# Attention by batch with transposed scores, and expert tiles started in three phases around the last batch's routing

## The chip, the cores and the metric

The kernel runs on one core of a Trainium2 chip. Its engines are TensorE (PE, with its weight loads listed as PEld), VectorE (DVE), ScalarE (ACT), GpSimd (POOL) and SyncE (SP), and they meet only at semaphores. The metric is the time of one execution on the device in microseconds; the median of three runs is given. All matrices are float32 unless a name ends in _b (bf16).

## The reference

Cross attention over 4 batches of 512 tokens (width 128, 16 heads of 8) with 77 context rows per batch, then a layer of 8 experts with 2 choices per token among 9 (the ninth returns the token itself):

```python
q = (query @ Wq + bq).reshape(b, nq, H, DH).transpose(0, 2, 1, 3)
scores = jnp.einsum('bhqd,bhkd->bhqk', q, k) / np.sqrt(DH)
scores = jnp.where(mask, -jnp.inf, scores)
w = jax.nn.softmax(scores, axis=-1)
attn = jnp.einsum('bhqk,bhkd->bhqd', w, v)
x = x + attn.transpose(0, 2, 1, 3).reshape(b, nq, H * DH) @ Wo + bo   # query = layernorm(x)
logits = xn @ router_w + router_b                                      # xn = layernorm(x)
probs = jax.nn.softmax(logits, axis=-1)
top_v, top_i = jax.lax.top_k(probs, TOP_K)
gates = jnp.sum(jax.nn.one_hot(top_i, E + 1) * top_v[..., None], axis=-2)
h = jax.nn.gelu(jnp.einsum('btd,edf->ebtf', xn, w1), approximate=False)
y = jnp.einsum('ebtf,efd->ebtd', h, w2)
x = x + jnp.einsum('bte,ebtd->btd', gates[..., :E], y) + gates[..., E:] * xn
```

## The kernel before

**Attention** goes by tiles of 128 tokens, 16 of them, four to a batch. For each tile PE writes the scores of 16 heads x 77 keys (1232 columns) into the four banks of ps_s (L774): K is block diagonal (kbd), so that four groups of 32 rows of the array work on four banks. DVE takes the maximum of each head in two halves of 616 columns (mx, L1058) and subtracts it (sc, L1062); ACT takes one exponential of 1232 columns (ex, L665). PE then transposes the 1232 columns in ten pieces (L798), ACT copies them out of PSUM in three parts (exT, L547), and ten products with a block diagonal V that holds a column of ones per head give both the weighted values and the sums (ps_av, L807). DVE multiplies with the reciprocals (L1081, L1082); one more transpose, one copy (L611) and one product with Wo (L786) follow, and DVE adds the residual tile by tile (L1070). The order is written out by hand: at tile i the engines do the scores of i, the transposes and products of i - 1 and the projection of i - 2. The batches in the middle run in a hardware loop.

**Routing** of a batch is spread over the four tiles of the next one: layer norm (ACT L591), transposes (L840), logits (L849), DVE's choice of two experts (choose, L1092 to L1107), ranks by triangular bf16 products (L861 to L867), slots (place, L1116 to L1128). POOL sends each tile's 128 rows twice, once per chosen expert, with an indirect DMA into the table slots in DRAM (send, L480), eight to a batch. The last batch is routed in two parts after its attention, with no other work beside it.

**Expert stage.** DVE works out a table of 40 tiles of 128 rows (L1190 to L1204: which expert, which row of slots). SP writes four pads of zero rows into slots and ACT four more (write_pad, L317 and L318), one per expert, at the end of its rows. SP then waits for the pads and for all sends, and loads tile after tile (xg, L364), eight buffers deep. For each tile PE transposes the rows (L917), multiplies with w1 (four products, each of two instructions, L926), ACT takes the gelu (L701), PE multiplies with w2 (L935), DVE scales by the gate (yg, L1222) and POOL scatters the result to pairs (L523). DVE also copies the expert's w1 to a fixed place (L1215) and the transposed rows out of PSUM (L1208). PE's order at step j is gather_t(j), up(j - 1), down(j - 2). At the end SP reads pairs back, DVE adds the two halves and the residual (L1246, L1247), and SP stores the result.

## Time and profile before

| what | value |
|---|---|
| median of 3 runs | 248.63 us (248.18 to 250.15) |
| profiled execution, span from first to last instruction | 257.3 us |
| busy: PE, DVE, POOL, ACT | 191.6, 156.0, 102.4, 102.0 us |
| start, to the first reduction of scores | 25.0 us |
| attention with routing of batches 0 to 2 | 25 to 135 us |
| routing of the last batch, table, pads, first load | 135 to 160.4 us |
| expert tiles | 160.4 to 242 us |
| last scatter, pairs, sum, store | 242 to 257.3 us |

The span of the one profiled execution is 8.7 us above the median of the runs without a profile; of the profiled execution only its span is recorded, with no time of its own around it. Busy shares are means over stages with different limits, so each stage is to be read by itself.

### The profile page before, as it was taken

Reading aid. Unit: us, or ns where it says so; the run is one execution under the profiler, and the core shown is the slowest. Engines: PE = TensorE matmul, PEld = TensorE weight load, DVE = VectorE, ACT = ScalarE, POOL = GpSimd, SP = SyncE. Lnnn points to the kernel's source line nnn. Section 1 sums busy time; section 2 is a strip of 40 time slices with the busy share of each in tenths; the row PEclk is TensorE's granted clock in tenths of the full one; section 3 lists DMA queues with packets and bytes.
Section 4 is the critical chain, followed back from the end, with each engine's and each line's share of the span. In section 5 each row is a group of like instructions: output and inputs, shape, how many; then the busy total and the mean of one; then the engine's idle time right before and its main releaser. Section 6 shows DMA issues by size and latency. Waiting matters only on the chain.

```text
span 257.3 us, 5658 instructions
## 1 busy us (share of the span) xinstructions
PE 191.6 (74%) x1467; PEld 169.9 (66%) x1468; DVE 156.0 (61%) x498; ACT 102.0 (40%) x210; POOL 102.4 (40%) x148
## 2 busy tenths in 40 slices
PE   1747899999986599849783200999999999999500
PEld 0516488778765587739782100899999999999500
DVE  2799968788883678938853650254554554554226
ACT  2411565678654476436653310122322322323100
POOL 8293001002047520782057479044554554554600
PEclk9999999999999589997978555599999999999955
DMA  3535892000001000110001031212222222210069
GB/s 98 159 122 215 263 309 83 4 0 0 4 20 44 9 0 0 37 36 0 0 28 50 21 103 50 61 47 74 59 68 64 71 62 68 62 52 11 3 218 271
DMA packets 20303, 18.30 MB, mean 71 GB/s; under 512 B 3255, under 2 KB 16752, under 8 KB 20287
## 3 DMA queue, kind: packets, MB, share of 16 engines
q1 hardware_dynamic: 16831, 13.98, 18.5%
q0 software_dynamic: 2304, 3.75, 4.7%
q10 hardware_dynamic: 1152, 0.37, 0.6%
q8 instruction: 8, 0.13, 0.2%
q14 instruction: 8, 0.07, 0.1%
HBM read 10.60 MB, written 8.50 MB: 74 GB/s over the span
## 4 chain that ended last, share of the span: by engine, by line
PE 48%; DVE 23%; issue 9%; DMA 6%; ACT 4%; another core or an unknown queue 4%; SPq 3%; POOL 1%; DVEq 0%; POOLq 0%; ACTq 0%
PE ps_s L926 14%; PE ps_av L807 8%; PE ps_av L935 7%; PE ps_o L935 6%; PE ps_t L798 5%; DVE mx L1058 4%; DVE sc L1062 3%; DMA pair_sb<-pairs 2%; PE ps_t L917 2%; DMA ctx_sb<-in_ctx 2%; DVE v_sb L1030 1%; PE ps_s L774 1%; DVE v_sb L1032 1%; SPq L317 1%
## 5 line engine op out<-in xcount | busy, mean ns | idle before, releaser
L523 POOL DMA_INDIRECT pairs<-yg,xg x40 | 39.1, 976 | 44.1 <-issue 22.7
L701 ACT ACTIVATE hT<-ps_s 128x512 f32<-128x512 f32 x40 | 23.9, 597 | 61.5 <-PE ps_s L926 61.5
L480 POOL DMA_INDIRECT slots<-rows,slot x32 | 31.7, 990 | 39.1 <-issue 18.3
L926 PE MATMUL ps_s<-xgT,w_now 128*128 128x128 f32 x320 | 44.4, 283 | 0.0
L807 PEld LDWEIGHTS ps_av<-vbd,exT 128*128 128x128 f32 x320 | 40.9, 205 | 2.4 <-issue 2.4
L807 PE MATMUL ps_av<-vbd,exT 128*128 128x99 f32 (+1 forms) x320 | 41.8, 286 | 0.8 <-issue 0.8
L926 PEld LDWEIGHTS ps_s<-xgT,w_now 128*128 128x128 f32 x320 | 40.5, 199 | 0.1
L1215 DVE COPY w_now<-w_sb 128x512 f32 x40 | 17.2, 429 | 21.5 <-issue 16.9
L798 PE MATMUL ps_t<-ident,ex 128*128 128x128 f32 x160 | 28.1, 314 | 0.1
L547 ACT COPY exT<-ps_t 128x384 f32<-128x384 f32 (+1 forms) x48 | 24.1, 514 | 7.5 <-PE ps_t L798 4.2
L1058 DVE TENSOR_REDUCE mx<-ps_s 128x8 f32<-128x616 f32 x32 | 25.4, 793 | 2.5 <-PE ps_s L774 1.9
L1062 DVE TENSOR_TENSOR sc<-ps_s,mx 128x616 f32<-128x616 f32 x32 | 25.6, 799 | 1.3
L665 ACT ACTIVATE ex<-sc 128x1232 f32<-128x1232 f32 x16 | 19.7, 1230 | 10.2 <-DVE sc L1062 10.1
L436 POOL TENSOR_TENSOR kbd<-kT,hm 128x308 f32<-128x308 f32 x4 | 2.8, 704 | 51.9 <-PE ps_s L774 46.8
L798 PEld LDWEIGHTS ps_t<-ident,ex 128*128 128x128 f32 x160 | 20.9, 160 | 2.6 <-ACT ex L665 0.8
L917 PE MATMUL ps_t<-ident,xg 128*128 128x128 f32 x40 | 11.5, 287 | 14.6 <-DMA xg<-slots 14.5
L935 PE MATMUL ps_av<-w_sb,hT 128*128 x160 | 22.2, 283 | 0.0
L935 PE MATMUL ps_o<-w_sb,hT 128*128 x160 | 21.5, 277 | 0.2 <-issue 0.2
L935 PEld LDWEIGHTS ps_av<-w_sb,hT 128*128 128x128 f32 x160 | 20.2, 198 | 0.2
L935 PEld LDWEIGHTS ps_o<-w_sb,hT 128*128 128x128 f32 x160 | 19.5, 192 | 0.4 <-issue 0.4
L774 PE MATMUL ps_s<-kbd,qT 32*128 32x308 f32 x128 | 16.7, 510 | 2.9 <-DVE sc L1062 1.6
L1208 DVE COPY xgT<-ps_t 128x128 f32<-128x128 f32 x40 | 11.4, 284 | 8.3 <-PE ps_t L917 8.3
(157 smaller groups left out, 239.9 us busy)
## 6 DMA issues: line engine op xcount, KB each, us to landing
xg<-slots SPq DMA_DIRECT2D x40, 65.0 KB
pairs<-zeros SPq DMA_DIRECT2D x4, 512.0 KB, 4.0
w_sb<-in_L_ffn_w SPq DMA_DIRECT2D x1, 2048.0 KB, 9.7
pair_sb<-pairs SPq DMA_DIRECT2D x3, 512.0 KB, 4.7
x_sb<-in_x SPq DMA_DIRECT2D x4, 256.0 KB, 6.7
out<-out_sb SPq DMA_DIRECT2D x3, 256.0 KB, 2.9
pairs<-yg,xg POOLq DMA_INDIRECT x40
slots<-rows,slot POOLq DMA_INDIRECT x32
```

What stands on the lines that cost most here:

```text
L480: pool.indirect_dma_start(slots, bass.IndirectOffsetOnAxis(ap=slot[k][:, t, c:c + 1], axis=0), rows[:, t, :], None, bounds_check=ROWS - 1, ...
L523: pool.indirect_dma_start(pairs, bass.IndirectOffsetOnAxis(ap=xg[:, u, D + 1:D + 2].bitcast(U32), axis=0), yg[:, u % 4, :], None, bounds_c ...
L547: act.copy(dst, src).then_inc(t_used, 1)
L665: act.activation(ex[:, t % 2, 0:HK], sc[:, t % 2, :], ACT.Exp).then_inc(ex_ready, 1)
L701: act.activation(hT[:, u % 2, :], ps_h[u % 2], ACT.Gelu).then_inc(h_used, 1)
L774: m = pe.matmul(ps_s[:, g, 0:GK], qT[r, P * t:P * (t + 1)], kbd[r, :, :].rearrange("p h k -> p (h k)"), start=True, stop=True)
L798: m = pe.transpose(ps_t[bank][:, P * (c - a):P * (c - a + 1)], ex[:, par, P * c:P * (c + 1)], ident[:, :])
L807: m = pe.matmul(ps_av[:, (DH + 1) * head0[c]:(DH + 1) * head0[c] + VC], exT[:, par, P * c:P * (c + 1)], v, start=c == 0, stop=c == NCH - 1 ...
L926: m = pe.matmul(ps_h[par][:, P * c:P * (c + 1)], w1_now[:, par, P * c:P * (c + 1)], xgT[:, par, :], start=True, stop=True)
L935: m = pe.matmul(ps_y[par], hT[:, par, P * c:P * (c + 1)], w2_sb[:, bass.ds(e + P * c, D)], start=c == 0, stop=c == FC - 1)
L1058: link(dve.tensor_reduce(m, s, AX.X, ALU.max))
L1062: dve.tensor_tensor(o.rearrange("p (g h k) -> p g h k", g=2, k=NK), s, m.rearrange("p (g h) -> p g h", g=2).unsqueeze(3) .to_broadcast([P, ...
```

## The change

The kernel is rewritten in most of its functions; the expert tile itself (gather_t, up, gelu, down, take_result, send_back) keeps its instructions.

- **Scores twice.** For each batch the scores are still computed with tokens on the partitions, but only to take their maxima (max_scores on PE into one pair of banks ps_m, top_scores on DVE). The maxima of a batch are split into three bf16 parts (split), transposed (max_out) and copied out (mT_out). Then score_t writes the scores of the whole batch transposed, keys on the partitions and 512 tokens in the free dimension, in three rounds of up to 103 rows of the 308 (4 heads x 77 keys) per group: first a bf16 product that puts minus the maximum into PSUM, then kbd times q on top. ACT's exponential writes exT straight from PSUM. The transposes of ex, their copies, and DVE's subtraction are gone.
- **Products by column groups.** attend multiplies exT (512 columns) with 32 columns of V for each of four groups, each to its own 32 partitions of one bank, and the same again with ones (den). inverse (ACT: Ln, Exp) and combine (DVE, one Newton step) give the transposed attention output; project and residual go by batch.
- **The start.** Context and weights come packed and transposed from the host side, constants come by DMA instead of from POOL; the batch's maxima of batch 0 are taken ahead of the loop.
- **Three phases.** The table is made in parts: tiles 0 to 7 after the routing of batches 0 and 1, tiles 8 to 15 after batch 2 (full tiles only), tiles 16 to 38 after batch 3 and the pads, which SP now writes alone (eight). NJ goes from 40 to 39. PE starts expert tiles right behind the attention of the last batch, whose remaining steps (combine, project, residual, norm, logits, choose, ranks, place, table, send) stand between expert tiles 1 to 8. xg has 16 buffers, yg has 8. All loops are unrolled.

The diff, cut to its core (a gap is marked by a line of three dots):

```diff
+NJ = NTOK * TOPK // P + E - 1
...
+NR = 3
+CUT = [0, 103, 206, 308]
...
+PHASES = [(0, 8), (8, 16), (16, NJ)]
+XR = 16
+YR = 8
...
-
-            sp.wait_ge(tab_ready, 1)
-            for e in range(E // 2):
-                write_pad(sp, e)
-            sp.wait_ge(tab_ready, 2)
-
...
+            for q, (a, z) in enumerate(PHASES):
+                for b in range(q + 2 if q < 2 else B):
+                    sp.wait_ge(sent[b], 16 * 2 * TT)
+                if q == 2:
+                    sp.wait_ge(pad_ready, 1)
+                    for e in range(E):
+                        row = sp.value_load(tab_pad[0:1, e:e + 1], min_val=0, max_val=DEAD - P)
+                        sp.dma_start(slots[bass.ds(row, P), :], padrows[:, :]).then_inc(pads_done, 16)
+                    sp.wait_ge(pads_done, 16 * E)
+                sp.wait_ge(tab_ready, q + 1)
+                for i in range(a, z):
+                    load(i)
...
+            for i in range(NJ):
+                send_back(i)
+                if i == 1:
+                    b = B - 1
+                    pool.wait_ge(stats2_ready, B)
+                    pool.wait_ge(rstd2_ready, 1)
+                    pool.tensor_tensor(rstd2[:, b * TT:NT], veps2[:, b * TT:NT], seed2[:, b * TT:NT],
+                                       ALU.pow).then_inc(rstd2_ready, 1)
+                if i == 2:
+                    prepare(B - 1)
+                if i == 3:
+                    pool.wait_ge(lgx_ready, B)
+                    pool.tensor_tensor(lex[:, :, :], r0[:, 0:TT * (E1 + 2)].rearrange("p (t e) -> p t e", t=TT),
+                                       lgx[:, :, :], ALU.pow).then_inc(lex_ready, 1)
+                if i == 5:
+                    send(B - 1)
+                if i == 24:
+                    identity(2)
+                if i == 30:
+                    identity(3)
...
+                for h in range(2):
+                    act.wait_ge(s_full, 2 * n + h + 1)
+                    act.activation(exT[0:w, n % ES, 2 * h:2 * h + 2, :], ps_s[0:w, 2 * h:2 * h + 2, :],
+                                   ACT.Exp).then_inc(s_free, 1)
...
+            for i in range(NJ):
+                gelu(i)
+                if i == 2:
+                    norm2(B - 1)
+                if i == 3:
+                    x2nT_out(B - 1)
+                if i == 4:
+                    logits_out(B - 1)
+                if i == 6:
+                    ranks_out(B - 1)
...
+            def max_scores(b, t):
+                for h in range(2):
+                    begin_m(f"d {b} {t} {h}")
+                    scores(b, t, h, ps_m).then_inc(m_full, 1)
...
+            def score_t(b, r):
+                n = NR * b + r
+                w = CW[r]
+                if r == 0:
+                    pe.wait_ge(mT_ready, b + 1)
+                if n:
+                    pe.wait_ge(s_free, 2 * n)
+                for g in range(G):
+                    pe.matmul(ps_s[0:w, g, :], ind_b[32 * g:32 * g + 12, CUT[r]:CUT[r + 1]],
+                              mT[32 * g:32 * g + 12, b % 2, :], start=True, stop=False)
+                for g in range(G):
+                    flat = kbd[32 * g:32 * g + 32, b, :, :].rearrange("p h k -> p (h k)")
+                    m = pe.matmul(ps_s[0:w, g, :], flat[:, CUT[r]:CUT[r + 1]], qT[32 * g:32 * g + 32, b % 3, :],
+                                  start=False, stop=True)
+                    if g % 2:
+                        m.then_inc(s_full, 1)
...
+            def attend(b, r):
+                n = NR * b + r
+                w = CW[r]
+                if r == 0:
+                    av, den = begin_v(f"av {b}"), begin_v(f"den {b}")
+                av, den = ps_v[v_use(f"av {b}")[0]], ps_v[v_use(f"den {b}")[0]]
+                pe.wait_ge(s_free, 2 * n + 2)
+                for g in range(G):
+                    i = pe.matmul(av[32 * g:32 * g + 32, :], vbd[0:w, r, b, g, :], exT[0:w, n % ES, g, :],
+                                  start=r == 0, stop=r == NR - 1)
+                if r == NR - 1:
+                    v_filled(i, f"av {b}")
+                for g in range(G):
+                    i = pe.matmul(den[32 * g:32 * g + 32, :], dbd[0:w, r, b, :], exT[0:w, n % ES, g, :],
+                                  start=r == 0, stop=r == NR - 1)
+                if r == NR - 1:
+                    v_filled(i, f"den {b}")
+                else:
+                    i.then_inc(av_rounds, 1)
+
...
+                score_t(b, 0)
+                if b == 0:
+                    fill_xn(1)
+                    fill_v(1)
+                    fill_q(1)
+                    fill_v(2)
+                    pe.wait_ge(bv4_ready, 1)
+                    v_filled(pe.matmul(begin_v("bo")[:, 0:D], bv4[:, :], wo_sb, start=True, stop=True), "bo")
+                    pe.wait_ge(kbd_ready, B)
+                    bank, k = v_use("q 1")
+                    pe.wait_ge(v_free[bank], k + 1)
+                if b >= 1:
+                    attend(b - 1, 1)
+                    attend(b - 1, 2)
                 for t in range(TT):
+                    if b + 1 < B:
+                        max_scores(b + 1, t)
+                    if t == 0:
+                        score_t(b, 1)
+                    if t == 1 and b >= 1:
+                        project(b - 1)
+                    if t == 1 and b + 2 < B:
+                        fill_xn(b + 2)
+                    if t == 2:
+                        score_t(b, 2)
+                    if t == 2 and b + 2 < B:
+                        fill_q(b + 2)
+                if b >= 1:
+                    fill_x2n(b - 1)
+                    logits(b - 1)
+                if b == 0:
+                    pe.wait_ge(dbd_ready, 1)
+                    pe.wait_ge(vbd_ready, NR)
+                attend(b, 0)
+                if b + 1 < B:
+                    max_out(b + 1)
+                if b >= 1:
+                    ranks(b - 1)
+                if b + 2 < B:
+                    bank, k = v_use(f"q {b + 2}")
+                    pe.wait_ge(v_free[bank], k + 1)
+            attend(B - 1, 1)
+            attend(B - 1, 2)
...
-                def transposes(p):
-                    number, bank = fill(kind, n, FILLS[f"T{t}"] + p)
-                    begin_fill(number)
-                    a, z = PIECES[p]
-                    for c in range(a, z):
-                        m = pe.transpose(ps_t[bank][:, P * (c - a):P * (c - a + 1)], ex[:, par, P * c:P * (c + 1)],
-                                         ident[:, :])
-                    m.then_inc(t_full, 1)
-
-                def products(p):
-                    number, _ = fill(kind, n, FILLS[f"T{t}"] + p)
-                    pe.wait_ge(t_used, number + 1)
-                    for c in range(*PIECES[p]):
-                        v = vflat[:, bass.ds((b * NCH + c) * VC, VC)]
-                        m = pe.matmul(ps_av[:, (DH + 1) * head0[c]:(DH + 1) * head0[c] + VC],
-                                      exT[:, par, P * c:P * (c + 1)], v, start=c == 0, stop=c == NCH - 1,
-                                      skip_group_check=True)
-                    return m
-
-                pe.wait_ge(ex_ready, i + 1)
-                transposes(0)
-                transposes(1)
-                if project_before:
-                    project(i - 1, (par + 1) % 2)
-                transposes(2)
-                if isinstance(i, int) and i == 0:
-                    pe.wait_ge(vbd_ready, 3)
-                else:
-                    pe.wait_ge(av_ready, i)
-                products(0)
-                if last_tile and kind != "last":
-                    number, bank = fill(kind, n, FILLS["q"])
-                    fill_q(number, bank, fill(kind, n, FILLS["xn"])[0])
-                products(1)
-                if last_tile and kind == "mid":
-                    ranks(n - 1)
-                products(2).then_inc(av_full, 1)
...
+            for i in range(NJ + 2):
+                if i < NJ:
+                    gather_t(i)
+                if 1 <= i < NJ + 1:
+                    up(i - 1)
+                if i == 2:
+                    project(B - 1)
+                if i == 5:
+                    fill_x2n(B - 1)
+                if i == 6:
+                    logits(B - 1)
+                if i == 8:
+                    ranks(B - 1)
+                if i >= 2:
+                    down(i - 2)
...
+            def split(b):
+                parts = [mpad[:, :, i, :] for i in range(3)]
+                m = mx[:, :].rearrange("p (a j) -> p a j", j=HG)
+                rest = [mrest[:, i, :].rearrange("p (a j) -> p a j", j=HG) for i in range(2)]
+                link(dve.tensor_copy(parts[0], m))
+                link(dve.tensor_tensor(rest[0], m, parts[0], ALU.subtract))
+                link(dve.tensor_copy(parts[1], rest[0]))
+                dve.tensor_tensor(parts[2], rest[0], parts[1], ALU.subtract).then_inc(split_ready, 1)
...
+            def combine(b):
+                av, den = ps_v[v_use(f"av {b}")[0]], ps_v[v_use(f"den {b}")[0]]
+                dve.wait_ge(r0_ready, b + 1)
+                wait_v_full(dve, f"den {b}")
...
-            def less_max(kind, n, t):
-
-                i = n * TT + t
-                par = t % 2
-                for half in range(2):
-                    dve.wait_ge(s_full, i * 2 + half + 1)
-                    s = ps_s[:, 2 * half:2 * half + 2, 0:GK].rearrange("p g (h k) -> p g h k", k=NK)
-                    m = mx[:, par, 8 * half:8 * half + 8]
-                    link(dve.tensor_reduce(m, s, AX.X, ALU.max))
-                    if half == 0 and (kind != "first" or t >= 2):
-                        dve.wait_ge(ex_ready, i - 1)
-                    o = sc[:, par, 2 * GK * half:2 * GK * (half + 1)]
-                    dve.tensor_tensor(o.rearrange("p (g h k) -> p g h k", g=2, k=NK), s,
-                                      m.rearrange("p (g h) -> p g h", g=2).unsqueeze(3)
-                                      .to_broadcast([P, 2, HG, NK]), ALU.subtract).then_inc(s_used, 1)
...
+                    if b + 1 < B:
+                        top_scores(b + 1, t)
+                    if t == 0 and b >= 1:
+                        combine(b - 1)
+                    if t == 1 and b >= 1:
+                        residual(b - 1)
+                    if t == 2 and b >= 1:
+                        refine2(b - 1)
+                if b + 1 < B:
+                    split(b + 1)
+                    mT_out(b + 1)
+                if b >= 1:
+                    choose(b - 1)
+                    place(b - 1)
+                if b == 2:
+                    table(0)
+                if b == 3:
+                    table(1)
...
+            for i in range(NJ + 2):
+                if i < NJ:
+                    if i == PHASES[phase_of(i)][0]:
+                        dve.wait_ge(tab_ready, phase_of(i) + 1)
+                    take_w1(i)
+                    take_rows(i)
+                if i >= 2:
+                    take_result(i - 2)
+                if i == 1:
+                    combine(last)
+                if i == 2:
+                    residual(last)
+                    ts = slice(last * TT, NT)
+                    dve.memset(seed2[:, ts], -0.5)
+                    link(dve.memset(r0[:, 0:TT * (E1 + 2)], float(np.e)))
+                    dve.tensor_scalar(veps2[:, ts], mv2[:, ts, 1], EPS, None, ALU.add).then_inc(rstd2_ready, 1)
+                if i == 3:
+                    refine2(last)
+                if i == 6:
+                    choose(last)
+                if i == 8:
+                    place(last)
+                    table(2)
```

## Rows read from the trace of the kernel before

**Rows 1.** Stretches of the span (busy us per engine, granted clock, DMA share, GB/s)
```profile
77.00:106.00 29.00, 23.74 (x180) 20.29 (x180) 19.88 (x63) 15.65 (x34) 12.35 (x18) 0.88 0.05 17
135.00:160.40 25.40, 3.62 (x22) 2.51 (x22) 9.99 (x61) 5.80 (x18) 17.72 (x23) 0.59 0.19 57
160.40:242.00 81.60, 80.49 (x680) 79.33 (x680) 38.62 (x119) 23.90 (x40) 37.92 (x40) 0.96 0.21 55
242.00:257.30 15.30, 0.00 (x0) 0.00 (x0) 5.93 (x11) 0.00 (x0) 1.68 (x2) 0.60 0.67 206
```

**Rows 2.** Chain that ended last: two pauses that no recorded instruction releases
```profile
80.26 5.39 another core or an unknown queue
...
110.65 4.01 another core or an unknown queue
```

**Rows 3.** Timeline of the start
```profile
15.67 1.41 PE L774 MATMUL ps_s<-kbd,qT 32*128 32x308 f32 x8 [1.04 <-ACT qT L552]
...
21.52 0.84 DVE L970 BATCH_NORM_STATS2 st<-x_sb 128x6 f32<-128x128 f32 x4
```

**Rows 4.** Groups by line and shape (busy us, mean ns of one, idle before)
```profile
L1058 DVE TENSOR_REDUCE mx<-ps_s 128x8 f32<-128x616 f32 x32 | 25.4, 793 | 2.5 <-PE ps_s L774 1.9 <-issue 0.3
...
L665 ACT ACTIVATE ex<-sc 128x1232 f32<-128x1232 f32 x16 | 19.7, 1230 | 10.2 <-DVE sc L1062 10.1
...
L1246 DVE TENSOR_TENSOR out_sb<-pair_sb 128x512 f32<-128x512 f32 x3 | 2.1, 691 | 6.9 <-DMA pair_sb<-pairs 6.9
```

**Rows 5.** Timeline of PE within a batch
```profile
43.27 1.05 PE L742 MATMUL ps_t<-xnT,wq_sb 128*128 128x512 f32 x2
...
45.79 0.80 PE L774 MATMUL ps_s<-kbd,qT 32*128 32x308 f32 x8
```

**Rows 6.** Timeline of DVE: routing of one batch, table of 40 tiles
```profile
96.92 0.19 DVE L1092 TENSOR_TENSOR lgx<-lg_sb,rb_sb 128x36 f32<-128x36 f32 x1
...
98.75 0.20 DVE L1106 TENSOR_TENSOR chosen<-oh 128x36 bf16<-128x36 f32 x1
...
147.67 0.16 DVE L1189 CAST tab_pad<-nextrow 128x8 int32<-128x8 f32 x1
...
151.18 0.18 DVE L1204 TENSOR_SCALAR tab_row<-jrow 128x40 int32<-128x40 f32 x1
```

**Rows 7.** Timeline of the expert stage: two neighbouring tiles on PE, one on DVE
```profile
200.02 0.27 PE L917 MATMUL ps_t<-ident,xg 128*128 128x128 f32 x1
...
201.06 0.43 DVE L1215 COPY w_now<-w_sb 128x512 f32 x1 [0.48 <-issue]
...
201.40 0.29 DVE L1208 COPY xgT<-ps_t 128x128 f32<-128x128 f32 x1
...
201.92 0.27 PE L917 MATMUL ps_t<-ident,xg 128*128 128x128 f32 x1
...
202.12 0.35 DVE L1222 TENSOR_SCALAR yg<-ps_av,xg 128x128 f32<-128x128 f32 x1 [0.43 <-PE ps_av L935]
```

**Rows 8.** Timeline of POOL: rows sent to the slots, the last tile sent back
```profile
76.72 0.97 POOL L480 DMA_INDIRECT slots<-rows,slot  x1 [0.30 <-issue]
78.00 0.98 POOL L480 DMA_INDIRECT slots<-rows,slot  x1 [0.30 <-issue]
...
243.12 0.97 POOL L523 DMA_INDIRECT pairs<-yg,xg  x1 [0.41 <-issue]
245.35 2.55 SPq L376 DMA_DIRECT2D pair_sb<-pairs  x5
```

**Rows 9.** Timeline of SP and ACT queues: pads, then the first seven loads
```profile
148.85 7.66 SPq L318 DMA_DIRECT2D slots<-padrows  x4
149.09 2.64 ACTq L318 DMA_DIRECT2D slots<-padrows  x3
...
158.54 7.47 SPq L364 DMA_DIRECT2D xg<-slots  x7
```

**Rows 10.** Chain that ended last: a load from its issue to its landing
```profile
159.68 1.74 DMA xg<-slots
```

1572 lines of the change are left out of this document (713 added, 859 removed).

## The prediction

> **What bounds the kernel now.** I read the stretches first [rows 1]. In a batch of attention (77 to 106 us) PE is busy 23.7 of 29.0 us and DVE 19.9: neither is full, so the chain between them sets the time. From 135 to 160.4 us PE works 3.6 us: the last batch is routed with nothing beside it, and this is the hole that the change aims at. From 160.4 to 242 us PE is full, a tile every 1.90 us [rows 7], and DVE needs 0.48 + 0.43 + 0.28 + 0.35 = 1.5 us of each 1.9 (the wait for the register before w_now, and the three instructions). Then the chain of what ended last: it holds two pauses of 5.4 and 4.0 us in which no recorded instruction releases anybody [rows 2]. They sum to 9.4, and the profiled span is 8.7 above the median of the timed runs. I therefore take the pauses for the profile's own: 257.3 - 9.4 = 247.9 stands for 248.6, and my sum, which has no such pauses, is compared with 247.9, with 0.7 added at the end.
>
> **The start.** Before, the first scores begin at 15.7 [rows 3]. The context transposes and the V product ahead of it go, and DVE writes the normalised rows: I put the first scores at 12.9. The first reduction starts at 14.1; eight of 0.79 [rows 4] and three groups of statistics (0.84 for four tiles [rows 3], with the aggregation 1.25) give 24.2; the second refinement, split, the transposes and the copy of the maxima some 3.3: batch 0's maxima are there at **27.5**.
>
> **Prices on PE.** A 512-column pass takes (1.05 - 0.19) / 2 = 0.43, where 0.19 is the time from a matmul's last column to its end; eight passes of 308 columns in four row groups take 0.80 - 0.19 = 0.61 [rows 5], where one after another they would take 8 x 0.26 = 2.1. So score_t costs 1.0 for kbd times q (0.61 x 512 / 308) and 0.25 for the bf16 part: 1.25. A half of max_scores has two groups: 0.75 until DVE sees it. attend uses column groups, which no row of this trace shows. Its bounds: as good as row groups, 2 x 1.0 = 2.0; one after another, 16 x 0.43 = 6.9. I take 2.0, as the row groups show the array's other direction at work, and keep 6.9 as a rival. The Trainium skill (TensorE: Matmul & The Clock Gate, part 3) has three column groups of 512 columns at 2.38 times one; by that attend would be some 2.9, and 12 of them 11 us more in all; no row here shows it.
>
> **A batch of attention after the change** (b = 2), from the copied maxima on. PE waits for choose of batch 0 (96.92 to 98.95, 2.0 [rows 6]) and does its ranks: 2.4. score_t 3.65, attend twice 7.65. Then the first two halves: ps_m is one pair of banks, so PE's fill of 0.75 and DVE's 0.79 take turns: 10.8. combine, three steps of 0.69 [rows 4]: 12.9. Two reductions with a fill between them: 15.3; residual with statistics 2.2: 17.5; two reductions 19.9; refine2 20.9; two reductions 23.3, split 24.2. Beside it the third score_t ends at 20.3, ACT's exponentials take 2 x 1.02 (1.23 x 1024 / 1232 [rows 4]), the norm 1.95, the transposes, their copy, the logits 2.3: 26.6. attend 2.0 and the maxima's transposes and copy 1.05: **29.6**. Batch 1 has no ranks to wait for but a q copy: 27.9. Batch 0, with V, q and xn of batch 1 ahead of the first exponential: 21.2. Batch 3 has no maxima: 2.4 + 1.25 + 4.0, inverse, exponentials, combine and project to 12.1, score_t and residual to 14.3, third exponential 17.0, norm and logits 21.6, choose 23.7, ranks and two attends **28.0**. So the expert tiles begin at 27.5 + 21.2 + 27.9 + 29.6 + 28.0 = **134.2**, where they began at 160.4 (151.0 without the pauses). What goes per tile (ten transposes, the copies, 1.6 us of subtraction) was real work, but the new chain has the maxima's turns in its place: the attention with its last routing gains 17 us, no more.
>
> **The expert stage.** PE's own work is 39 x 1.90. But DVE, in order, carries the last batch between tiles. DVE is in table(1) until 1.9 after PE's first tile. Nine tile steps at 1.2 are 10.8, seven results 2.5, combine 2.1, residual 2.8, choose 2.3, place 1.6, and some 5.8 of waits: POOL's power behind two scatters (1.6), gelu and down behind the norm (1.4), down behind project, logits and ranks (2.8). The slots are there at 1.9 + 22.1 + 5.8 = 29.8. Behind place stands table(2) (3.7 for 40 tiles [rows 6]), during which PE idles. POOL then sends eight times, one each 1.28, the last landing 2.2 after its start [rows 8]: 41.1. Only then does SP write pads, eight on one queue. Price of one: 1.07 as a load (7.47 / 7 [rows 9]), or 2.1 as the pads of before (7.66 for four starts and the ACT queue at the same time); I take 1.2, since the slow ones coincide with ACT's pads, which are gone: 50.7. Landing 1.7, then a load of 0.6 + 1.74 [rows 10]: tile 16 is there at 54.7. PE could have taken it at 46: it **stands still for 8 to 9 us**. From there 23 x 1.90 + 2.8 = 46.5, and one tile's time (1.9) for a clock that has fallen in the pause, as it has to 0.59 from 135 to 160.4 [rows 1]: 103.1, against 81.6 now. Everything that hides sends and pads of the last batch is 15 tiles of 1.9; the waits above have used it up before they start.
>
> The Trainium skill (DMA: Bandwidth & Descriptors, on issuing engines) says that DMAs from several engines share the same 16 DMA engines, so that a second issuer saves only issue time; by that, moving four pads from ACT to SP costs just four issues, 4.8 of my 9.6. The rows speak rather for two issuers being slower each (2.1 against 1.07 [rows 9]), and the sum would be the same.
>
> **The end** is unchanged, 15.3 [rows 1]. identity of batches 2 and 3 lies between scatters in POOL's slack (1.28 of 1.90).
>
> **The sum.** 134.2 + 103.1 + 15.3 = 252.6, and 0.7: **253.3**, 1.9% slower. Under 1% a measurement here hardly tells from no change.
>
> **Rivals.**
> 1. *The chain loosens* (27%). Before, a batch takes (29.0 - 5.4) / 19.9 = 1.2 times its busiest engine. After, DVE has 17.2 us of work in a batch and PE some 18 to 19. With 1.2 times 18.5, batches 1 to 3 would take 22.2 and not 28.5 on average: 19 us less, and a start that is 3 us shorter: **231**. It needs PE to fill ps_m while DVE is still busy elsewhere. Against it: the two halves of one tile can't overlap, and attends, score_t and norm stand in line.
> 2. *Pads stay slow* (17%), slower than before: eight at 2.1 and not 1.2 move tile 16 by 7 us: **260**. It decides from 1.2 us a pad up. For it: the rows of before. Against: two issuers then, one now.
> 3. *Column groups do not overlap* (7%): 4.9 more for each of 12 attends, little of it hidden since three of them stand in the chain of every batch: about **305**.
> 4. *The phases don't start early* (7%): if sends or table of batches 1 and 2 are late, PE waits at tile 0 or 8. Sends of batch 1 end some 17 us into the last batch, well ahead of its 28; I add 3 to 5 us: **257**.
>
> **How the numbers follow.** The forecast has 42%; around it I allow 246 to 260 (start and batches 1.5 us each, pads from 1.07), of which 6% are faster by over 1%, 12% within it, 24% slower. With the rivals: faster 6 + 25, within 1% 12 + 2, slower 24 + 17 + 7 + 7, rounded to 0.31, 0.14, 0.55. The range 231 to 264 leaves out rival 3 and the far half of rival 1.
>
> **What the new profile would show.** The first expert transpose near 134 (rival 1: under 120). A gap on PE before the 17th tile, with SP's pads in it and a load as what ends it: 8 us, or 15 under rival 2. A smaller gap near tile 9 while DVE makes the table. attend's 16 passes within 2 us, or 7. DVE waiting for PE and PE for DVE in turns at each pair of maxima, and DVE busy well under 20 us a batch. If PE has no gap of over 3 us ahead of tile 16, the step of the pads is wrong; if a batch takes under 25 us, that of the turns is; if pauses like those two are in no run without a profile, my basis holds.

## The result, and the profile after

| | before | after |
|---|---|---|
| median | 249.39 us (4 runs, 248.18 to 254.4) | 289.26 us (4 runs, 287.85 to 290.3) |
| ratio | 1 | 1.158 (1.149 to 1.168) |
| span of the profiled execution | 257.3 us | 286.4 us (288.45 in all) |

The change makes the kernel 16% slower. I had forecast 253.3 us, with a range from 231 to 264. Medians and ranges here hold every execution; the ratios leave out those that took over 1.5% longer than the quickest of the same kernel.

The page of after: span, busy shares, and the clock in 40 slices of 7.2 us.

```profile
span 286.4 us, 4468 instructions
PE 201.5 (70%) x1299; PEld 133.9 (47%) x1299; DVE 131.8 (46%) x463; ACT 76.7 (27%) x135; POOL 108.8 (38%) x133
...
PEclk9995585559795796555955977996697799999955
```

The stretches of after, beside [rows 1]: busy us by engine, granted clock, DMA share, GB/s. The cuts lie at the ends of the four copies of maxima (mT), the first expert transpose, the transpose of tile 16 and the end of PE's work (rounded; the table of the miss has them exactly).

```profile
0.00:28.10 28.10, 12.85 (x52) 6.29 (x52) 18.57 (x70) 5.31 (x12) 9.15 (x24) 0.87 0.68 225
28.10:61.50 33.40, 27.65 (x118) 12.07 (x118) 10.68 (x21) 11.41 (x18) 4.93 (x4) 0.60 0.22 62
61.50:93.70 32.20, 25.56 (x146) 11.31 (x146) 12.33 (x31) 11.00 (x18) 0.86 (x3) 0.78 0.00 1
93.70:129.00 35.30, 26.14 (x146) 11.72 (x146) 15.43 (x55) 10.39 (x18) 12.23 (x16) 0.68 0.04 14
129.00:161.10 32.10, 22.82 (x149) 8.33 (x149) 17.61 (x97) 10.59 (x20) 12.87 (x18) 0.66 0.12 32
161.10:221.00 59.90, 37.31 (x280) 35.76 (x277) 27.27 (x112) 13.68 (x25) 38.39 (x34) 0.84 0.17 52
221.00:270.00 49.00, 48.83 (x414) 48.30 (x414) 23.91 (x69) 14.33 (x24) 28.40 (x33) 0.95 0.19 51
270.00:286.40 16.40, 0.36 (x4) 0.17 (x2) 6.03 (x11) 0.00 (x0) 1.94 (x2) 0.61 0.64 192
```

Read the clock column first. From 28 to 161 us it is 0.60 to 0.78, where before had 0.88 in a batch with one of its two pauses [rows 1] and the full clock in the 29 us of attention ahead of them:

```profile
43.00:72.00 29.00, 28.17 (x238) 23.30 (x237) 23.89 (x75) 21.20 (x44) 1.52 (x4) 1.00 0.01 2
```

The clock has two levels, 1.2 and 2.4 GHz, so 0.60 means that it stood at the lower one for four fifths of batch 0. The miss, term by term:

| term | forecast | measured | miss |
|---|---|---|---|
| batch 0's maxima there | 27.5 | 28.1 | +0.6 |
| batch 0 | 21.2 | 33.4 | +12.2 |
| batch 1 | 27.9 | 32.2 | +4.3 |
| batch 2 | 29.6 | 35.4 | +5.8 |
| batch 3, to the first expert transpose | 28.0 | 32.0 | +4.0 |
| tile 16 after the start of the tiles | 54.7 | 59.5 | +4.8 |
| from there to PE's end | 48.4 | 49.8 | +1.4 |
| the end | 15.3 | 16.0 | +0.7 |
| sum | 252.6 | 286.4 | +33.8 |

27 of 34 us lie in the attention. What the level does to one operation is seen where it changes within a batch. Timeline of PE in after: start, duration, then the name; each row is eight passes in four column groups.

```profile
89.44 1.94 PE L671 MATMUL ps_v<-exT,vbd 103*32 103x512 f32 x8
91.15 1.74 PE L676 MATMUL ps_v<-exT,dbd 103*32 103x512 f32 x8
...
98.31 1.58 PE L671 MATMUL ps_v<-exT,vbd 103*32 103x512 f32 x8
99.72 1.03 PE L676 MATMUL ps_v<-exT,dbd 103*32 103x512 f32 x8
100.58 1.04 PE L671 MATMUL ps_v<-exT,vbd 102*32 102x512 f32 x8
101.44 1.03 PE L676 MATMUL ps_v<-exT,dbd 102*32 102x512 f32 x8
```

An attend is two such rows: 100.58 to the start of the next work at 102.40 is 1.8 us, 89.44 to 92.83 is 3.4 us. The work is the same. The clock fell between 85 and 86 us, behind waits of PE for the last maxima (0.90 us) and the normed rows (0.25); after the wait for the chosen experts (2.55 us, to 95.8) the work was at the low level again, and the high one came back between 99 and 100 us, in the middle of score_t and the attends, which follow each other without a gap from 96.0 on. So the question for the experiments: is the attention long because PE's waits take its clock away, or are the waits themselves the length and the clock only their shadow?

In the expert stage, the timeline of POOL, where the last batch's exponentials are made with a power:

```profile
186.09 7.43 POOL L434 TENSOR_TENSOR lex<-r,lgx 128x44 f32<-128x44 f32 x1 [2.93 <-DVE lgx L971]
193.72 1.04 POOL L417 DMA_INDIRECT pairs<-yg,xg  x1 [0.20 <-issue]
195.06 0.98 POOL L417 DMA_INDIRECT pairs<-yg,xg  x1 [0.31 <-issue]
196.35 0.98 POOL L388 DMA_INDIRECT slots<-rows,slot  x1 [0.30 <-issue]
```

and what PE waited for at two places there (in brackets the idle time and its releaser), then the chain into tile 16:

```profile
200.15 2.08 PE L813 MATMUL ps_s<-xgT,w_now 128*128 128x128 f32 x8 [8.75 <-DVE xgT L1103]
220.63 0.48 PE L805 MATMUL ps_m<-cf,xg 128*128 128x128 f32 x1 [6.54 <-DMA xg<-slots]
```

```profile
216.38 1.69 DMA slots<-padrows
218.09 0.28 SPq L306
218.41 0.15 SPq L306
218.56 0.05 issue
218.81 1.77 DMA xg<-slots
```

DVE stands in place until the power is done, makes table(2) behind it, and PE stands behind DVE for 8.75 us, more than at tile 16; I had forecast a gap there that is smaller than that at tile 16. Then the forecast's gap: eight sends to 205.4, landed at 207.7, eight pads of 1.08 each to 216.4, landing 1.69, load 1.77, and PE idle for 6.54 us ahead of tile 16.

### The profile page after: what moved, and what is told of

The parts are those of the page before. It is cut to its first block, busy times and chain, and to the rows that moved or that the text cites. A ratio compares the mean times of both kernels' runs of the same rounds, so it can differ in the third digit from the quotient of the medians.

```text
span 286.4 us, 4468 instructions
## 1 busy us (share of the span) xinstructions
PE 201.5 (70%) x1299; PEld 133.9 (47%) x1299; DVE 131.8 (46%) x463; ACT 76.7 (27%) x135; POOL 108.8 (38%) x133
## 4 chain that ended last, share of the span: by engine, by line
PE 50%; DVE 18%; issue 12%; DMA 6%; ACT 5%; POOL 4%; SPq 3%; DVEq 1%; POOLq 0%; ACTq 0%
PE ps_s L813 9%; PE ps_s L823 7%; PE ps_m L627 6%; PE ps_v L671 5%; PE ps_s L658 5%; PE ps_v L676 4%; DVE mx L868 4%; DMA exT<-pairs 2%; PE ps_m L714 2%; PE ps_v L687 2%; PE ps_v L614 2%; ACT rows L509 2%; PE ps_v L620 2%; POOL pairs L417 2%; PE ps_v L607 1%
## 5 line engine op out<-in xcount | busy, mean ns | idle before, releaser
L417 POOL DMA_INDIRECT pairs<-yg,xg x39 | 38.5, 987 | 35.2 <-DVE yg L1115 29.1
L823 PE MATMUL ps_s<-w_sb,hT 128*128 x312 | 43.9, 287 | 0.0
L823 PEld LDWEIGHTS ps_s<-w_sb,hT 128*128 128x128 f32 x312 | 40.5, 203 | 0.1
L627 PE MATMUL ps_m<-kbd,qT 32*128 32x308 f32 x108 | 28.4, 612 | 16.6 <-DVE mx L868 15.8
L868 DVE TENSOR_REDUCE mx<-ps_m 128x8 f32<-128x616 f32 x27 | 21.6, 799 | 39.7 <-PE ps_m L627 36.2
L486 ACT ACTIVATE exT<-ps_s 103x1024 f32<-103x1024 f32 (+1 forms) x24 | 23.4, 1020 | 26.9 <-PE ps_s L658 26.7
L1115 DVE TENSOR_SCALAR yg<-ps_s,xg 128x128 f32<-128x128 f32 x39 | 13.6, 349 | 28.3 <-PE ps_s L823 28.3
L377 POOL COPY rows<-rows 128x512 f32<-128x512 f32 x4 | 2.5, 616 | 54.7 <-ACT rows L509 54.7
L658 PE MATMUL ps_s<-qT,kbd 32*103 32x512 f32 (+1 forms) x96 | 23.1, 861 | 0.0
L671 PE MATMUL ps_v<-exT,vbd 103*32 103x512 f32 (+1 forms) x96 | 18.2, 842 | 0.0
L676 PE MATMUL ps_v<-exT,dbd 103*32 103x512 f32 (+1 forms) x96 | 16.6, 774 | 0.0
L805 PE MATMUL ps_m<-cf,xg 128*128 128x128 f32 x39 | 11.3, 295 | 6.5 <-DMA xg<-slots 6.5
```

Of the source, the lines that this page charges most:

```text
L417: pool.indirect_dma_start(pairs, bass.IndirectOffsetOnAxis(ap=xg[:, i % XR, D + 1:D + 2].bitcast(U32), axis=0), yg[:, i % YR, :], None, bo ...
L486: act.activation(exT[0:w, n % ES, 2 * h:2 * h + 2, :], ps_s[0:w, 2 * h:2 * h + 2, :], ACT.Exp).then_inc(s_free, 1)
L627: m = pe.matmul(o[:, g, 0:GK], qT[rows, b % 3, P * t:P * (t + 1)], kbd[rows, b, :, :].rearrange("p h k -> p (h k)"), start=True, stop=True)
L658: m = pe.matmul(ps_s[0:w, g, :], flat[:, CUT[r]:CUT[r + 1]], qT[32 * g:32 * g + 32, b % 3, :], start=False, stop=True)
L671: i = pe.matmul(av[32 * g:32 * g + 32, :], vbd[0:w, r, b, g, :], exT[0:w, n % ES, g, :], start=r == 0, stop=r == NR - 1)
L676: i = pe.matmul(den[32 * g:32 * g + 32, :], dbd[0:w, r, b, :], exT[0:w, n % ES, g, :], start=r == 0, stop=r == NR - 1)
```

## The experiments

Ratios are to the kernel before, run on the same chip in the same group; before took 258.6, 252.4, 259.4 and 253.0 us in the four groups. A batch runs from one copy of the maxima to the next, times and clock from the profile.

**1 and 2. Filler at TensorE's waits** (the second with twice the products at each). The kernel uses all of PSUM, so the products go to places that are rewritten before they are read: a bank of ps_s whose scores are consumed, the next destination, the second bank of ps_m between two uses.

```
+            def warm(o, n):
+                for _ in range(n):
+                    pe.matmul(o[:, 0:256], ones_b[:, :], ind_b[:, 0:256], start=True, stop=True)
...
+                    if h:
+                        pe.wait_ge(s_free, 2 * (NR * (b - 1) + (0, 1, 1, 2)[t]) + 1)
+                        warm(ps_s[:, 0, :], 4)
                     begin_m(f"d {b} {t} {h}")
...
+                warm(o, 4 if b < B - 1 else 0)
                 pe.wait_ge(row_ready, b + 1)
```

> Filler bf16 products of 256 columns (four each, eight before the ranks) stand ahead of TensorE's waits in the attention: the second half of each pair of maxima, the transposed maxima, the normed rows, the transposed rows, the chosen experts. They write PSUM that is overwritten before it is read. Theory A (the attention of after is long because TensorE is at its half clock for most of it: granted 0.66 to 0.74 between 28 and 162 us, and the same 16 passes of attend take 3.4 us there against 1.72 us where it is full): the clock of that stretch rises above 0.8 and the kernel loses 8 to 20 us. Theory B (the turns between TensorE and VectorE alone set the length, the low clock is only their shadow): a filler adds work to a chain that waits, so the time stays within 2 us or grows by up to 4 us, whatever the clock does.

> The same with twice the filler (eight products, sixteen before the ranks), some 0.9 us of it at the full clock and 1.7 us at the half one at each wait. Theory A: the clock of 28 to 162 us above 0.9; 15 to 25 us off the kernel if the fillers don't overhang the waits; where they do (0.9 us of filler in a gap of 0.9 us) they give a few us of it back. Theory B: slower than the light filler, 0 to 8 us over the kernel after.

Measured: 284.07 us, ratio 1.102 (1.092 to 1.111), and 287.04 us, 1.105 (1.095 to 1.115). The four batches of the light one:

```profile
28.50:57.30 28.80, 26.22 (x138) 12.86 (x138) 10.64 (x20) 11.32 (x18) 4.92 (x4) 0.82 0.24 65
57.30:84.10 26.80, 22.55 (x170) 10.39 (x170) 12.32 (x30) 11.00 (x18) 0.87 (x3) 1.00 0.00 1
84.10:115.20 31.10, 26.60 (x182) 13.03 (x182) 15.82 (x56) 10.50 (x18) 12.27 (x16) 0.84 0.05 16
115.20:147.70 32.50, 24.69 (x176) 11.32 (x176) 17.28 (x96) 10.60 (x20) 13.12 (x18) 0.79 0.12 31
```

In batch 1 PE has 24 products more than in after (170 against 146) and is busy 22.6 us instead of 25.6, in a batch that takes 26.8 instead of 32.2. In the two profiles the attention is 14 us shorter (119.2 against 133.0), and theory B, by which added work shortens nothing, is out. The kernel gains less than its attention: 4 to 5% by the ratios of the two runs of after (1.158 and 1.145), but only 2% by the times themselves, 284.07 against 289.26, which are from different chips. Its expert stage is 7 us longer than in after (132.0 against 125.3), and PE stands still for 3.9 of them in one of the pauses of the last section. The full dose reaches no more than the light one, below theory A's 15 to 25 us: its batches 2 and 3 took 35 us each at 0.85 and 0.81, each with a pause of 2.8 or 2.7 us that no recorded instruction ends (last section).

**3 and 4. The two stalls of the expert stage, one at a time.** The pads ahead of the wait for the sends:

```
-                for b in range(q + 2 if q < 2 else B):
-                    sp.wait_ge(sent[b], 16 * 2 * TT)
                 if q == 2:
                     sp.wait_ge(pad_ready, 1)
                     for e in range(E):
...
+                for b in range(q + 2 if q < 2 else B):
+                    sp.wait_ge(sent[b], 16 * 2 * TT)
+                if q == 2:
                     sp.wait_ge(pads_done, 16 * E)
```

> The eight pad writes of the last phase are issued before SyncE waits for the sends of the last batch, not behind them. Both theories: the stall of 6.5 us ahead of tile 16 shrinks. The pads took 8.7 us of issues behind the sends plus 1.7 us of landing; without them the loads start about 10 us earlier than in after, which is more than the stall, so 6 to 7 us come off if what follows is set by TensorE, less if the result transfers of GpSimd are next in line (then 2 to 4 us).

and the exponentials on ScalarE, behind ranks_out(B - 1), with the power on GpSimd taken out:

```
                 if i == 6:
                     ranks_out(B - 1)
+                    router_exp(B - 1)
```

> The last batch's exponentials (128x44) go back to ScalarE's Exp, between two gelus; GpSimd's power of 7.43 us goes. Theory A and B alike: the slots are ready 5 to 7 us earlier, VectorE's wait in place (8.75 us of TensorE idle behind it) falls to 2 to 4 us, two table loads of some 1.3 us each come on ScalarE between the gelus: 3 to 6 us faster. If the stall only moves to tile 16, whose rows wait for the sends, most of it still comes off, since the sends start earlier by the same amount.

Measured: 296.71 us, ratio 1.138 (1.130 to 1.147), and 294.24 us, 1.139 (1.132 to 1.146); some 5 us each against after's 1.158. Against the 1.145 of the second run of after (experiment 5) neither gain is clear of the noise. In the first, PE had no gap at tile 16. But another stood before it, and no recorded instruction ends it; the chain of waits and PE's row:

```profile
211.08 8.01 another core or an unknown queue
```

```profile
220.88 2.08 PE L814 MATMUL ps_s<-xgT,w_now 128*128 128x128 f32 x8 [4.93 <-DVE xgT L1104]
```

Such pauses, like those of [rows 2], are in both kernels and not in after; I come back to them in the last section. This one takes back in full what the pads gave, and they make the two single gains less sure still. In the second, ScalarE needed 1.28 + 0.24 + 1.28 us for table, exponentials and table back, instead of 7.43, and PE's wait fell from 8.75 to 3.57 us, as expected; tile 16 did not come earlier (61.5 us after the first tile, 59.5 in after), with a wait of PE for such a pause, 3.9 us, and one behind the table loads, 1.8 us, on the way. The gain of both together is seen in experiment 8, which has no pause.

**5. After once more,** to have it beside the next three.

> The kernel after, unchanged, beside the kernels of this group, since the kernel before took 258.6 us beside the first four against 249.4 beside after: a ratio of 1.15 to 1.17 again by every theory, and batches of 32 to 36 us at a granted clock of 0.6 to 0.8.

289.22 us, ratio 1.145 (1.139 to 1.150); batches of 32.7, 36.3, 34.6 and 34.2 us at 0.60, 0.65, 0.70 and 0.70.

**6. Maxima bank by bank.**

```
+                both = name[0] == "d" and M_USES[n - 1][0] == "d"
                 if n:
-                    pe.wait_ge(m_free, n)
+                    pe.wait_ge(m_free, n - 1 if both else n)
...
-                    begin_m(f"d {b} {t} {h}")
-                    scores(b, t, h, ps_m).then_inc(m_full, 1)
+                    for g in range(2):
+                        begin_m(f"d {b} {t} {h} {g}")
+                        rows = slice(32 * (2 * h + g), 32 * (2 * h + g) + 32)
+                        pe.matmul(ps_m[:, g, 0:GK], qT[rows, b % 3, P * t:P * (t + 1)],
+                                  kbd[rows, b, :, :].rearrange("p h k -> p (h k)"), start=True,
+                                  stop=True).then_inc(m_full, 1)
```

> The maxima by single PSUM banks: TensorE fills bank 1 while VectorE reduces bank 0 (one matmul and one reduce of 308 columns each), instead of both filling and reducing a pair of banks in turn. No filler. Theory A (the low clock costs most): the waits of 0.9 to 2.2 us behind each pair go, the clock of 28 to 129 us rises, and both together give 8 to 16 us. Theory B (only the turns cost): some 0.7 us less for each of 24 halves that stand in the chain, but VectorE pays about 0.1 us more for each half: 5 to 12 us, and the clock has no say; the passes of attend stay at 3.4 us. Theory C (what stands in line besides the maxima sets the batch: score_t, attends, combine, norm, logits, choose): under 4 us.

289.31 us (285.3 to 290.8) against 289.22 (287.9 to 292.6): no clear gain. In a pair, the two products stand in different rows of the array and run at once: the four passes of a half took 0.79 us. Released one by one they took 1.17 at the full clock (71.8 us). VectorE's halves then followed each other every 1.36 us instead of 1.69 (at 67 and at 69 us of the two traces), and the kernel shows nothing of it. Batch 1 took 32.8 us at 0.75, among the others, so by the time alone this is theory C's "under 4". It doesn't say that the maxima are cheap, as the next run shows.

**7. No maxima after batch 0.** max_scores and top_scores are left out for batches 1 to 3.

> It leaves out part of the computation: the maxima of batches 1 to 3 (24 halves of scores on TensorE and their reductions on VectorE); batch 0's maxima are subtracted in every batch. It prices the maxima with their turns. By the forecast's own batches (each half 1.6 us of turns, partly beside other work) 24 halves come to at most 38 us, of which some 20 to 25 come off. Theory A: TensorE then has even less to do between its waits, so the clock stays at 0.6 to 0.75 and batches 0 to 2 end at 22 to 26 us each, 20 to 28 us off the kernel. Theory B: 30 us or more come off. Theory C: under 12 us.

259.98 us, ratio 1.031 (1.027 to 1.036): 29 us less than after in the same group, more than theory A allowed and just under B's 30.

```profile
28.40:46.90 18.50, 13.37 (x86) 6.53 (x86) 7.22 (x12) 11.01 (x18) 4.93 (x4) 0.89 0.35 98
46.90:72.60 25.70, 18.68 (x114) 7.89 (x114) 5.98 (x22) 10.99 (x18) 0.87 (x3) 0.75 0.00 1
72.60:101.60 29.00, 19.34 (x114) 7.41 (x114) 9.87 (x48) 10.15 (x18) 11.77 (x16) 0.63 0.05 16
101.60:135.90 34.30, 24.83 (x148) 8.88 (x148) 19.19 (x104) 10.71 (x20) 15.01 (x20) 0.70 0.12 34
```

The 24 halves cost 14, 11 and 6 us in the three batches. Theory A had the clock at 0.6 to 0.75 and the batches at 22 to 26 us: batch 0 came to 18.5 us at 0.89, so less work between the waits did not lower the clock there, and batch 2 still took 29.0 at 0.63. So the maxima's turns are not the only waits that go with the low clock. A kernel without them still doesn't beat before.

**8 and 9. Everything together.**

> Bank by bank, the light filler at the waits for the transposed maxima, normed rows, transposed rows and chosen experts (none at the maxima), the pads ahead of the sends, the exponentials on ScalarE, twelve result buffers instead of eight, and GpSimd's sends of the last batch one result later. Theory A: the clock of the attention above 0.85, the expert tiles begin near 140, the stalls before tiles 10 to 16 fall from 15 to about 6 us: 25 to 32 us less than after, a ratio of 1.02 to 1.06 to the kernel before. Theory B: 12 to 18 us less. Theory C: 8 to 14 us, all of it in the expert stage.

> The light filler of the first experiment (four products at the second half of each pair of maxima too) on the kernel with pads ahead of the sends, exponentials on ScalarE, twelve result buffers and the later send. The last combination without a filler at the maxima (and by single banks) had a ratio of 1.07 to the kernel before: attention until 155.6, and 112.4 us from the first expert tile to the end. Theory A (the clock): the attention ends near 148 as with the light filler alone, the clock there is 0.8 to 0.9, the expert stage is the same 112 to 114: 7 to 9 us less, a ratio of 1.03 to 1.05. If the gains of filler and order are the same slack counted twice, it stays at 1.06 to 1.08.

The first: 269.8 us, ratio 1.070 (1.064 to 1.075), 19 us less than after, between the theories: A wanted 25 to 32 us and a clock above 0.85, and the four batches had 0.67, 0.83, 0.75 and 0.83; B allowed 12 to 18. The tiles began at 155.6, where A had 140, and took 112.4 us to the end, against 124.4 in after of the same group: 12 us from pads, exponentials, buffers and the later send, 9.4 of them up to tile 16, which came 49.2 us after the first tile and not 58.5, without a wait. The second: 278.35 us, ratio 1.070 (1.062 to 1.078), where I expected 1.03 to 1.05. Its first two batches were quick, 25.7 us at 0.86 and 27.6 at 0.94; the last two were not, 35.0 at 0.80, with a pause of 3.4 us in it, and 35.2 at 0.71; and its expert stage took 124 us with a pause of 6.5 us in it. The first version had none, so the two are not cleanly comparable.

**10 and 11. The last batch routed ahead of the tiles,** the other half of the change undone (the calls for batch B - 1 moved in front of the loops over tiles on all engines).

> The other half of the change undone: the last batch is combined, routed and sent in one piece ahead of the expert tiles, as in the kernel before (its exponentials on ScalarE, as there); tiles 0 to 15 then run while it is sent and padded. From the end of the last attends some 16 to 18 us pass until place is done, with TensorE nearly idle; then 16 tiles of 1.9 and the table of 3.6. Sends, pads and the load take 10.3 + 2.3 + 8.7 + 1.7 + 2.3 = 25 us beside them, so tile 16 doesn't wait: it comes 50 to 53 us after the end of the attends, where it came 59.8 after it in after. Routing between the tiles is then worth less than nothing: 7 to 10 us faster than after, ratio 1.11 to 1.13. If the waits between tiles were cheap and only power and pads cost, this is slower than after or within 2 us of it.

> Routing first with the light filler in the attention, the pads ahead of the sends and twelve result buffers. The parts should add: 13 us from the filler, 7 to 10 from the order, nothing from the pads, which are hidden already: 20 to 23 us less than after, ratio 1.06 to 1.08. Against the kernel with filler and routing between tiles it tells which order is better once both have no pad stall: by the sums 3 to 5 us in favour of routing between the tiles.

293.9 us, ratio 1.134 (1.127 to 1.141), where I expected 1.11 to 1.13; and 280.42 us, with executions from 275.8 to 286.7 beside 259.4 of before, too far apart for a ratio (1.06 to 1.11). In the first, 52.6 us pass from the last copy of maxima to the first tile, and 105.9 from there to the end: 158.5, against 157.4 in after, but with a pause of 4.2 us in it. Tile 16 has no gap and comes 57.2 us after the end of the attends (166.5), against 59.5 in after; I had written 50 to 53. The waits of PE that remain are those of the routing in one piece, and table(2):

```profile
170.58 2.04 PE L677 MATMUL ps_v<-w_sb,avT 128*128 128x128 f32 x8 [4.13 <-DVEq L908]
178.15 1.08 PE L684 MATMUL ps_v<-cf,rows 128*128 128x128 f32 x4 [5.53 <-ACT rows L502]
...
199.30 1.64 PE L807 MATMUL ps_s<-xgT,w_now 128*128 128x128 f32 x8 [4.13 <-issue]
```

With the filler the two orders have spans of 276.1 and 276.4 us, with pauses in both. So these runs show no gain of the routing between the tiles over the routing in one piece, and none the other way that is clear of the pauses. The three phases let tiles start before the last batch's rows are in place, and either order lets 16 tiles cover its sends.

**12. V later in batch 0.** fill_v(1), fill_v(2) and the product for bo behind the first and second pair of maxima, on PE and DVE alike.

> Only batch 0 is changed: the V products for the second and third range of keys and the product for bo are issued behind the first and second pair of batch 1's maxima instead of ahead of them. In after they stand in the chain with 1.7 + 0.9 us on TensorE and 2 us on VectorE ahead of the first reduction. If the 33 us of batch 0 (21.2 forecast) are a chain of fixed work ahead of the first maxima, 3 to 5 us go from batch 0 and from the kernel. If they are the low clock (0.60 there), the work is only moved and under 2 us go.

305.98 us, ratio 1.169 (1.156 to 1.182), against 1.158 and 1.145 of after: at least it got no faster, and both expectations are missed. Batch 0 shows more:

```profile
28.40:66.60 38.20, 32.03 (x118) 13.79 (x118) 9.53 (x21) 11.51 (x18) 4.93 (x4) 0.51 0.18 50
```

The same instructions, 4.8 us more than in after and 5.8 more than in experiment 10, whose batch 0 is that of after and ran in the same group (32.4 at 0.62); PE is at its lower level throughout. A chain of fixed work would have become shorter. That the solid work between the waits had kept up what clock there was is my reading; no second run tests it.

**13 and 14. Filler in one batch, and more of it at the long waits.**

> The light filler in one batch alone, the one between the second and the third copy of maxima (61 to 94 us in after): four products at the second half of each of its pairs, at the transposed maxima, the normed rows and the transposed rows. Theory A (the clock): this batch alone rises from a granted clock of 0.65 to 0.78 to 0.95 or more and falls from 32 to 36 us to 27 or 28; the batches ahead of it and behind it stay at 32 to 37 us and 0.60 to 0.70. In the sum 5 to 8 us off the kernel. If something else in the filler kernels made them faster (another order at the waits for freed scores, a faster chip), the gain isn't bound to this batch.

> The version with filler and order, with ten products instead of four at the long waits (transposed maxima, normed rows, transposed rows; twenty before the ranks), since its last two batches were still at 0.80 and 0.71 of the full clock and took 35 us each. Over the batches measured so far a batch's time falls by some 3 us for each 0.1 of clock. If the clock of these two rises to 0.9, 3 to 5 us each come off, less about 1 us for filler that overhangs: ratio 1.04 to 1.06 to the kernel before. If the filler overhangs as in the full dose, it stays at 1.07 or gets worse.

The executions of these two spread too far for a ratio: 282.0 to 290.7 us and 264.1 to 276.5, beside 253.0 of before. The batches of the first:

```profile
28.50:60.10 31.60, 26.05 (x122) 11.54 (x122) 10.62 (x20) 11.41 (x18) 4.93 (x4) 0.68 0.22 61
60.10:88.90 28.80, 25.72 (x171) 12.06 (x170) 12.34 (x31) 11.01 (x18) 0.87 (x3) 0.88 0.00 1
88.90:122.60 33.70, 24.44 (x146) 11.34 (x146) 15.50 (x55) 10.39 (x18) 11.93 (x16) 0.71 0.05 15
122.60:154.70 32.10, 22.84 (x148) 8.28 (x148) 17.59 (x96) 10.59 (x20) 12.96 (x18) 0.66 0.12 32
```

Only the batch with filler is at 0.88 and under 29 us, short of the 0.95 and the 27 to 28 us that I expected; its neighbours are at 0.68 and 0.71, as in kernels without filler. That is within one execution, so the chip doesn't explain it. The added wait for freed scores stands in the same batch as the filler; it can only hold PE back, but a kernel with that wait and without the products was not run. In the second kernel the last two batches came to 31.2 and 31.9 us at 0.89, 3 to 4 us less each, as theory A says, while batch 1, with 42 products more than in after, fell to 0.72 and took 36.0: the filler makes the high level likelier, not certain. Its execution of 264.1 us (1.04 times before, the only one in the range that I expected) had a mean clock of 0.894, that of 276.5 us (1.09) 0.837. No version beats before.

The batches of all profiles, each as time at granted clock (without those of experiment 7, and batch 3 without 10 and 11, which route it otherwise):

| batch | in order of clock |
|---|---|
| 0 | 38.2 at 0.51; 33.4 and 32.7 at 0.60; 32.4 at 0.62; 31.2 at 0.67; 31.6 at 0.68; 33.1, 32.7 and 32.8 at 0.69; 28.8 at 0.82; 25.9 at 0.85; 26.1 and 25.7 at 0.86; 25.7 at 0.87 |
| 1 | 36.3 at 0.65; 34.0 (three) and 33.9 at 0.70; 36.0 at 0.72; 32.8 at 0.75; 32.2 at 0.78; 30.8 at 0.83; 28.7 and 28.8 at 0.88; 28.7 and 27.6 at 0.94; 26.8 at 1.00 |
| 2 | 35.4 at 0.68; 34.6 and 35.0 at 0.70; 33.7 at 0.71; 34.3 and 34.0 at 0.75; 31.1 at 0.84; 31.2 at 0.89; with a pause in it: 36.8 (two) at 0.67; 37.9 at 0.68; 34.9 at 0.76; 35.0 at 0.80; 34.9 at 0.85 |
| 3 | 32.0, 32.1 and 34.8 at 0.66; 34.2 at 0.70; 30.9 at 0.83; 31.9 at 0.89; with a pause in it: 34.8 at 0.66; 37.5 at 0.68; 34.2 at 0.70; 35.2 at 0.71; 32.5 at 0.79; 35.2 at 0.81 |

## Why the prediction was wrong

**The step that failed is "Prices on PE".** Each price there is read from rows at the full clock, and the batches add them up as if the chain they form would run at it. I used the clock at one place only, one tile's time after the stall. I named turn-taking between PE and DVE as what sets a batch, and did not ask what turn-taking does to PE's clock, though [rows 1] show it fall to 0.59 in the one stretch where PE has little to do. Measured: 0.60 to 0.78 in all four batches, and PE's steps in the chain up to twice their price: an attend 3.4 us where I took 2.0 (89.44 to 92.83), score_t 2.3 where I took 1.25 (96.0 to 98.3).

**How much is the clock.** Batch 1 at 1.00 took 26.8 us, forecast 27.9: the steps themselves were sized well. For batches 0 and 2 I have no time at the full clock. Straight lines through their times without a pause in the table above give 22.0 and 28.5 us at 1.00, an estimate, where I had 21.2 and 29.6; single batches lie up to 1.6 us off these lines. Batch 3 seems not to follow, but in experiment 14 its 31.9 us at 0.89 hold filler that PE worked off while what comes next was ready:

```profile
124.32 1.25 PE L603 MATMUL ps_m<-ind_b,ones_b 128*128 128x256 bf16 x10
...
142.80 2.33 PE L603 MATMUL ps_m<-ind_b,ones_b 128*128 128x256 bf16 x10
...
147.76 2.36 PE L603 MATMUL ps_m<-ind_b,ones_b 128*128 128x256 bf16 x20
149.95 0.17 PE L729 MATMUL ps_m<-chosen,upper_b 128*128 128x9 bf16 x1
```

The first holds up score_t by 1.1 us, the second the logits by 1.2 (their rows were there at 143.63), the third the ranks by 1.9 (the chosen experts were there at 148.03). Without these 4.2 us it is 27.7, where I had 28.0. So no batch is far from its sum at the full clock, and by these estimates the whole miss of the four batches, 26 us, goes with the clock within a few us. That the clock makes the time, and not only the time the clock, rests on experiments 1 and 13, where products that nobody needs raised the one and shortened the other.

**The turns** were there as forecast: VectorE waits 36 us for the maxima's scores and TensorE 16 us for VectorE's reductions, summed over 27 halves. By the run without maxima, 24 of these halves with their products and reductions cost 29 us of the kernel: that is the price, in this form, of knowing the maxima ahead of the subtraction in PSUM.

**Column groups** overlap: 1.8 us for an attend at the full clock, where I took 2.0. Rival 3 is out. The start of one row of eight passes to the next is 0.86 us (100.58 to 101.44): two passes of 512 columns at 0.43 [rows 5], so four groups cost what one does. The figure that I gave from the Trainium skill (TensorE: Matmul & The Clock Gate, part 3) is a speedup of three groups, 2.38, so that three take 3 / 2.38 = 1.26 times one, an estimate; my 2.9 us is 6.9 / 2.38, which lays the speedup of three groups on four. The trace is better than either. The sum did not use it. The rule of the Trainium skill that would have mattered is in the same page, part 1: TensorE's clock is gated by how busy the engine has lately been, and half speed is where it rests. This case's trace agrees where TensorE is idle for long (0.61 in the last 16.4 us of after, 0.59 in the hole of before [rows 1]), and I left it out.

**The expert stage.** The pads cost 1.08 each (1.2 taken), rival 2 is out; the load 1.77 (1.74). The gap at tile 16 was 6.5 us, not 8 to 9, since PE was later there itself, 53 us after the first tile and not 46. Mis-sized was POOL's power: I had no row for it and counted 1.6 us of waiting for power and scatters, it took 7.43 for 128x44 and 1.06 for 128x4. With it on ScalarE, PE's wait behind DVE was 5.2 us shorter, about the 4.8 by which tile 16 was late; that tile 16 then comes earlier by as much is not shown by itself, only together with the early pads (experiment 8).

**Rival 1** (the chain loosens, 231 us) was the opposite of what happened; rival 4 (phases start late) did not occur: PE waited 3.0 us behind its first two transposes for DVE, which was in table(1) until 1.5 us after the first (1.9 in the sum).

**The basis** held by luck. I took the two pauses of [rows 2] for the profile's own, and compared without them. After has none in its profile and before took 249.4 beside it, so the comparison was right. But in two later groups all seven executions of before took 257.7 to 260.9 us, profiled or not, and there the traces of the other kernels hold such pauses: the reason that I gave was wrong (last section).

## What to carry to other kernels

When a change turns a dense stage into a chain in which TensorE and another engine take turns, price TensorE's steps at both clock levels, and ask of each stretch whether TensorE keeps working through it; a busy share read at the low clock counts every step at up to twice its work. Look at the granted clock around the waits in the trace of before: the change may spread such waits over the whole kernel. Useful work between the waits can be worth more than its place in the chain suggests, and moving it away can cost more than it saves, as one run here suggests (experiment 12).
